# A decoder layer on one core: attention scores in four row groups of TensorE, the shared network by pairs of tiles, the expert loop three blocks deep

## The chip, the cores and the metric

The kernel runs on one core of a Trainium2 chip. The metric is the device time of one execution in microseconds (us), as the median of three runs. A core has five engines that run their own in-order programs and meet at semaphores: TensorE (PE) for matrix products, VectorE (DVE), ScalarE (ACT), GpSimd (POOL) and SyncE (SP), which issues transfers. Operands lie in SBUF; matrix products are written to eight banks of PSUM, each 128 partitions by 512 fp32 values.

## The reference

One layer on x of shape 8 x 128 x 256, with a context of the same shape. Cut to what matters:

```python
# 1. causal attention with low-rank queries and keys, 16 heads of 16 (2 of them rotary), per sequence of 128
h   = layernorm(x)
cq  = layernorm(h @ W_dq) * q_w + q_b            # 128 wide
ckv = layernorm(h @ W_dkv) * kv_w + kv_b         # 170 wide
q   = concat(cq @ W_uq, rope(cq @ W_qr))         # 14 + 2 heads
k   = concat((ckv @ W_ukv)[..., :224], rope(h @ W_kr))
v   = (ckv @ W_ukv)[..., 224:]
x   = x + softmax(mask(q @ k.T / 4)) @ v @ W_o.T
# 2. cross attention, 2 heads of 128; the scores are summed over the 8 sequences
Q, K, V = layernorm(x) @ Wh, ctx @ Wh, ctx @ Wh
A   = maximum(abs((Q @ K.T / sqrt(128) * decay).sum(axis=0)), 1)
x   = x + (relu(layernorm(x) @ Wg) * groupnorm(A @ V)) @ Wo
# 3. 16 experts of width 176, top 2 of each token's softmax, and a shared network of width 352
f   = layernorm(x);  p = softmax(f @ gate.T);  w, idx = top_k(p, 2)
x   = x + sum_k w_k * swiglu(f @ w_gu[idx_k]) @ w_dn[idx_k] + swiglu(f @ s_gu) @ s_dn
```

## The kernel before

A token tile is one sequence of 128 tokens (T = 128, B = 8 tiles, D = 256, which makes KD = 2 pieces of 128). Every engine has one program, written out by hand; the order of the work is the order of the calls in it, and waits on counted semaphores join the engines. A name such as `bank` stands for any PSUM bank.

**Attention.** The main loop of the PE program runs over the tiles i and does four chunks (NC = 4) of four heads (CH = 4). A chunk has three steps, a chunk or two apart: `scores` (L506), one product of K = 128 rows by 512 columns whose moving operand `kbd` is a block-diagonal spread of the keys of four heads, made by POOL's `expand` (L378); `prob_transpose` (L513), four transposes; `weigh_values` (L523), four products in which the transposed probabilities `prT` are the stationary operand and the 17 columns of `v_s` (16 values and a column of ones, which gives the softmax denominator) move. Between them DVE scales and masks the scores into `sc_s` (L1197) and takes the row maximum (L1200), and ACT does the exponentials (L939) and copies the transposed probabilities out of PSUM (L932). Interleaved are the steps of the tiles ahead and behind: `front_transpose` (L459) and `front_project` (L467) of tile i+2, `latent_transpose` (L472), `keys_values` (L483) and the query product (L485), `qk_transpose`, then `out_transpose` (L537) and `out_project` (L544) of tile i-1 or i-2, and for the cross attention `cross_transpose`, `cross_queries` (L559) and `cross_scores` (L567), which sums over all tiles in one bank. `ctx_part` makes the context's keys and values ahead of the loop. `gates` (L600) are the relu gates, in pairs of tiles q.

**Mixing.** After the last `cross_scores`, DVE applies the decay, `cross_mix(q)` multiplies by the context's values, group norm and gates follow on DVE, ACT and POOL, `cross_out` projects, and `cross_residual` adds x1 by a product with the identity. `router` makes the logits.

**Routing.** DVE finds the top two of 16 experts by a row of small operations from L1370 to `mb` (L1388); PE counts the pairs, DVE and POOL (L426) work out slots and rows. Each expert's rows are padded to blocks of 128; the program has 31 blocks, and the reference's inputs fill 25 of them. Meanwhile PE runs the shared network for the first six tiles (EARLY = 6): `shared_gate` (L747), `shared_up` (L753), `shared_transpose` (L762), `shared_down` (L771).

**Expert loop.** For each block POOL gathers 128 rows by an indirect transfer (L441), PE transposes them (L805), multiplies by the expert's weights (L821), transposes the hidden rows (L813) and multiplies down (L828); DVE copies the result (L1457), and POOL scatters it to `expert_out` in device memory (L446). After the loop PE does the last two tiles of the shared network, SP waits until all 31 blocks are scattered, and then loads each tile's two expert rows (L353):

```python
for r in range(RB):
    sp.wait_ge(dma_scattered[r], 16 * len(range(r, BLOCKS, RB)))
for t in range(B):
    sp.dma_start(yg[t], expert_out[0:SLOTS, :]...)   # L353, each tile's two rows
```

DVE weighs and adds them (L1495), and ACT's queue stores the output.

## Time and profile before

| | before |
|---|---|
| time, median of three runs | 334.25 us (333.32 to 335.49) |
| span of the profiled execution | 318.4 us |
| around the span (median less span) | 15.85 us |
| PE busy | 287.7 us, 90% of the span |
| DVE busy | 177.9 us, 56% |
| ACT busy | 136.5 us, 43% |
| POOL busy | 120.3 us, 38% |
| chain that ended last | PE 63%, DVE 15%, issue 9%, POOL 5%, DMA 4% |

The profile lists no time of its own for the profiled execution beside its span; the median of the runs stands for it. The span is what the engines' instructions cover, from the first to the last; the time of a run is longer by what lies around it. The chain is followed back from the last instruction to what released each step, so a share of it is time in which that engine set the end.

### The profile page before, as it was taken

Reading aid. Unit: us, or ns where it says so; the run is one execution under the profiler, and the core shown is the slowest. Engines: PE = TensorE matmul, PEld = TensorE weight load, DVE = VectorE, ACT = ScalarE, POOL = GpSimd, SP = SyncE. Lnnn points to the kernel's source line nnn. Section 1 sums busy time; section 2 is a strip of 40 time slices with the busy share of each in tenths; the row PEclk is TensorE's granted clock in tenths of the full one; section 3 lists DMA queues with packets and bytes.
Section 4 is the critical chain, followed back from the end, with each engine's and each line's share of the span. In section 5 each row is a group of like instructions: output and inputs, shape, how many; then the busy total and the mean of one; then the engine's idle time right before and its main releaser. Section 6 shows DMA issues by size and latency. Waiting matters only on the chain.

```text
span 318.4 us, 4990 instructions
## 1 busy us (share of the span) xinstructions
PE 287.7 (90%) x1492; PEld 209.9 (66%) x1493; DVE 177.9 (56%) x474; ACT 136.5 (43%) x363; POOL 120.3 (38%) x122
## 2 busy tenths in 40 slices
PE   2988798998999999999989899988999999999971
PEld 1645566676777677787877567656677777777750
DVE  1345666467587878556426873984433443334336
ACT  2555575536567575756631536321122222222220
POOL 1123333305133335051001730044677777776510
PEclk9999989587999999999999999999999999999995
DMA  7999872000000001000100012001323333333157
GB/s 225 261 332 369 248 185 88 2 0 0 2 0 3 1 0 30 2 1 3 45 1 2 0 66 68 0 0 37 98 92 108 99 109 102 102 99 99 49 176 252
DMA packets 20396, 26.72 MB, mean 84 GB/s; under 512 B 2640, under 2 KB 18138, under 8 KB 20378
## 3 DMA queue, kind: packets, MB, share of 16 engines
q1 hardware_dynamic: 16250, 17.31, 18.2%
q0 software_dynamic: 2976, 8.13, 8.6%
q10 hardware_dynamic: 1152, 1.05, 1.0%
q8 instruction: 10, 0.16, 0.2%
q14 instruction: 8, 0.07, 0.1%
HBM read 20.32 MB, written 6.16 MB: 83 GB/s over the span
## 4 chain that ended last, share of the span: by engine, by line
PE 63%; DVE 15%; issue 9%; POOL 5%; DMA 4%; ACT 2%; SPq 0%; DVEq 0%; POOLq 0%; ACTq 0%
PE bank L821 12%; PE bank L828 8%; PE bank L506 5%; PE bank L523 5%; PE bank L483 4%; PE bank L513 3%; PE bank L544 3%; PE bank L813 2%; PE bank L805 2%; DVE qk L1205 2%; PE bank L467 2%; DVE lat L1228 2%; PE bank L600 2%; POOL rs L371 2%; DMA cv_s<-expert_out 2%
## 5 line engine op out<-in xcount | busy, mean ns | idle before, releaser
L932 ACT ACTIVATE prT<-bank 128x512 f32<-128x512 f32 (+1 forms) x63 | 30.8, 489 | 74.8 <-PE bank L813 54.9
L939 ACT ACTIVATE pr_s<-sc_s,mx 128x128 f32<-128x128 f32 x128 | 40.8, 392 | 12.6 <-DVE mx L1200 12.6
L821 PE MATMUL bank<-gu_s,bxT 128*128 x124 | 41.9, 460 | 0.0
L1457 DVE COPY kbd<-bank 128x256 f32<-128x256 f32 x31 | 13.2, 425 | 42.8 <-PE bank L828 42.8
L366 POOL TENSOR_TENSOR rs<-ve,halfpow 128x1 f32<-128x1 f32 x16 | 8.8, 551 | 72.7 <-DVE ve L1177 72.7
L446 POOL DMA_INDIRECT expert_out<-kbd,prT x31 | 30.6, 986 | 15.0 <-DVE kbd L1457 7.7
L506 PE MATMUL bank<-kbd,qkT 128*128 128x512 f32 x64 | 36.0, 648 | 0.0
L441 POOL DMA_INDIRECT qx_s<-ffn_in,prT x31 | 30.1, 972 | 12.7 <-issue 7.3
L523 PEld LDWEIGHTS bank<-v_s,prT 128*128 128x128 f32 x256 | 32.2, 197 | 0.7 <-issue 0.7
L523 PE MATMUL bank<-v_s,prT 128*128 128x17 f32 x256 | 31.9, 258 | 0.3
L378 POOL TENSOR_TENSOR kbd<-qkT,tab 128x1024 f32<-128x1024 f32 x16 | 30.3, 1896 | 4.6 <-ACT qkT L932 4.6
L828 PE MATMUL bank<-dn_s,prT 88*128 x124 | 31.8, 379 | 0.0
L1197 DVE SCALAR_TENSOR_TENSOR sc_s<-bank,tabb 128x512 f32<-128x512 f32 x32 | 22.0, 687 | 14.4 <-PE bank L506 14.4
L513 PEld LDWEIGHTS bank<-tab,pr_s 128*128 128x128 f32 x128 | 17.3, 151 | 18.3 <-issue 17.9
L821 PEld LDWEIGHTS bank<-gu_s,bxT 128*128 128x128 f32 x124 | 21.2, 190 | 6.7
L1200 DVE TENSOR_REDUCE mx<-sc_s 128x4 f32<-128x512 f32 x32 | 21.9, 686 | 1.1
L828 PEld LDWEIGHTS bank<-dn_s,prT 88*128 88x128 f32 x124 | 21.1, 190 | 1.8
L371 POOL TENSOR_TENSOR rs<-ve,halfpow 128x2 f32<-128x2 f32 x8 | 5.6, 699 | 42.3 <-DVE ve L1220 42.3
L513 PE MATMUL bank<-tab,pr_s 128*128 128x128 f32 x128 | 20.7, 288 | 0.0
L483 PE MATMUL bank<-wkv_s,ckvT 85*128 85x480 f32 x32 | 16.4, 638 | 0.0
L771 PE MATMUL bank<-kbd 128*128 128x256 f32 (+1 forms) x48 | 12.1, 387 | 2.9 <-DVE x_s L1344 2.2
L467 PE MATMUL bank<-wm_s,xT 128*128 128x362 f32 x32 | 12.7, 522 | 1.2 <-ACT xT L932 1.0
(172 smaller groups left out, 492.7 us busy)
## 6 DMA issues: line engine op xcount, KB each, us to landing
gu_s<-in_w_gu SPq DMA_DIRECT2D x8, 704.0 KB, 10.4
dn_s<-in_w_dn SPq DMA_DIRECT2D x4, 704.0 KB
qx_s<-in_ctx_in SPq DMA_DIRECT2D x2, 512.0 KB, 7.5
ffn_in<-x_s SPq DMA_DIRECT2D x4, 256.0 KB, 2.1
cv_s<-expert_out SPq DMA_DIRECT2D x4, 256.0 KB, 3.9
gu_s<-expert_out SPq DMA_DIRECT2D x4, 256.0 KB, 5.4
out<-x_s ACTq DMA_DIRECT2D x8, 128.0 KB, 2.3
sgu_s<-in_s_gu_d SPq DMA_DIRECT2D x1, 704.0 KB, 6.7
```

Source lines behind the costliest of these rows:

```text
L378: nc.gpsimd.tensor_tensor(kbd[:, b % 2, g, :, :], qkT[:, b % 2, 2 + g, :].unsqueeze(1).to_broadcast([128, 8, T]), tab[:, C_HEAD:C_HEAD + 8 ...
L441: pool.indirect_dma_start(bx[:, i % RB, :], None, ffn_in[:], bass.IndirectOffsetOnAxis(ap=idx[:, 0, i:i + 1], axis=0)).then_inc(dma_gather ...
L446: pool.indirect_dma_start(expert_out[:], bass.IndirectOffsetOnAxis(ap=idx[:, 1, k:k + 1], axis=0), by[:, k % RB, :], None).then_inc(dma_sc ...
L483: last = mm(bank[3][:, 0:NOPE + D], ckvT[:, b % 2, k, :], wkv_s[:, k, :], start=k == 0, stop=k == 1)
L506: mm(o, qkT[:, b % 2, g, :], kbd[:, b % 2, g, h0:h0 + CH, :], start=True, stop=True).then_inc(pe_scores, 1)
L513: last = tr(bank[2][:, h * T:(h + 1) * T], pr_s[:, n % 2, h, :], idf)
L523: last = mm(bank[6][:, hh * (DH + 1):(hh + 1) * (DH + 1)], prT[:, n % 2, h, :], v_s[:, b % 3, hh, :], start=True, stop=True)
L821: last = mm(bank[2 + par][:, 0:2 * I], bxT[:, par, k, :], gu_s[:, k, bass.ds(e, 1), :], start=k == 0, stop=k == KD - 1)
L828: last = mm(bank[4 + par][:, 0:D], bhT[:, par, k, :], dn_s[:, k, bass.ds(e, 1), :], start=k == 0, stop=k == 1)
L932: copy = lambda o, i: nc.scalar.activation(o, i, ACT.Copy)
L939: last = nc.scalar.activation(pr_s[:, n % 2, h, :], sc_s[:, n % 2, h, :], ACT.Exp, bias=mx[:, n % 2, h:h + 1])
L1197: V.scalar_tensor_tensor(sc_s[:, n % 2, :, :], s, DH ** -0.5, maskb.unsqueeze(1).to_broadcast([128, CH, T]), ALU.mult, ALU.add).then_inc(d ...
```

## The change

- Scores: the 128 rows of queries and keys are taken as four groups of 32 rows. `kbd` spreads keys over two heads instead of eight and is made by DVE with the scale in it (`qk_out`), and a tile's scores are eight products of 32 rows by 256 columns, in four banks. The causal mask is put into the banks ahead of them by a bf16 product with the identity (`mask`). DVE only takes the row maximum from PSUM; ACT's exponentials read PSUM and give the denominators by `accum_out`.
- `weigh_values` has `v_s` as the stationary operand (32 columns, in one of four column groups) and the probabilities move, so its result comes out transposed. The reciprocals of the denominators are spread by POOL, transposed by PE (`rden_transpose`) and multiplied in. `out_transpose` is gone.
- x and the context also come transposed from the host; the front layer norm is folded into its weights (`weight_mean`). `cross_queries` is gone, since the context's keys are multiplied by Wh·Wh^T (`wh_square`). Half of the context's keys and values are made in tiles 0 and 1.
- `cross_scores` of all tiles stand behind the last tile; `gates` of pairs 0, 1 and 2 stand in the last two tiles, and those of pair 3 around the mixing. `cross_residual` is gone, DVE adds x1.
- Router: one column-tiled group of products (`routers`), a copy, two transposes; the top two are taken from the logits.
- Shared network: by pairs of tiles, hidden values made transposed, 256 columns per product, no transposes. Pairs 0 to 2 are done ahead of the loop, a third of pair 3 after block 14, the rest after the loop.
- Expert loop: written out, hidden rows two blocks and the down product three blocks behind `expert_up`; the copy of the result on ACT.
- SP waits only for the scatters of the blocks in use before it loads the token rows, and stores the outputs.

The core of the diff:

```diff
-                h0 = (c % 2) * CH
-                o = bank[n % 2][:].rearrange("p (h k) -> p h k", h=CH)
-                mm(o, qkT[:, b % 2, g, :], kbd[:, b % 2, g, h0:h0 + CH, :], start=True, stop=True).then_inc(pe_scores, 1)
+            def mask(b, r):
+                if b:
+                    pe.wait_ge(act_exp, NC * (b - 1) + r + 1)
+                mm(score_bank(r)[:].rearrange("p (h k) -> p h k", h=CH), idb, maskb.unsqueeze(1).to_broadcast([128, CH, T]),
+                   start=True, stop=False, skip_group_check=True)
+
+            def scores(b):
+
+                pe.wait_ge(dve_qk_T, b + 1)
+                for g in range(2):
+                    for r in range(NC):
+                        rows = slice(32 * r, 32 * r + 32)
+                        last = mm(score_bank(r)[:, g * 2 * T:(g + 1) * 2 * T].rearrange("p (h k) -> p h k", h=2),
+                                  qkT[rows, b % 2, g, :], kbd[rows, b % 2, g, :, :], start=False, stop=g == 1,
+                                  skip_group_check=True)
+                last.then_inc(pe_scores, 1)
...
-                    last = mm(bank[6][:, hh * (DH + 1):(hh + 1) * (DH + 1)], prT[:, n % 2, h, :],
-                              v_s[:, b % 3, hh, :], start=True, stop=True)
+                    v0 = (4 * half + h) * 2 * DH
+                    v0 = VB - DH + v0 if par else v0
+                    last = mm(bank[6][2 * DH * h:2 * DH * (h + 1), half * T:(half + 1) * T],
+                              v_s[:, b % 3].rearrange("p a n -> p (a n)")[:, v0:v0 + 2 * DH], prT[:, n % PR, h, :],
+                              start=c == 0, stop=c == NC - 1, skip_group_check=True)
...
+            def rden_transpose(b):
+                pe.wait_ge(pool_rden_spread, b + 1)
+                for k in range(KD):
+                    last = mm(bank[6][:, (KD + k) * T:(KD + k + 1) * T], rdx[:, k * T:(k + 1) * T], idf,
+                              start=False, stop=False, is_transpose=True, skip_group_check=True)
+                last.then_inc(pe_rden_T, 1)
...
+            def shared_up(q, c, halves=(0, 1)):
+
+                n, r = SC * q + c, shared_rows(c)
                 pe.wait_ge(act_ffn_in_T, q + 1)
...
+                for j in halves:
                     for k in range(KD):
+                        last = mm(shared_bank(q, c)[0:r, 2 * j * T:2 * (j + 1) * T],
+                                  sgu_s[:, k, j * SI + c * 128:j * SI + c * 128 + r],
+                                  xfT[:, k, 2 * q:2 * q + 2, :].rearrange("p b t -> p (b t)"), start=k == 0, stop=k == KD - 1)
...
+            for i in range(2, BLOCKS):
+                hidden_transpose(i - 2)
+                expert_up(i)
+                if i + 2 < BLOCKS:
+                    block_transpose(i + 2)
+                if i >= 3:
+                    expert_down(i - 3)
+                if i + 1 < BLOCKS:
+                    read_expert(i + 1)
+                if i == MID:
+                    shared_up(PAIRS - 1, 0)
...
                 for h in range(CH):
-                    last = nc.scalar.activation(pr_s[:, n % 2, h, :], sc_s[:, n % 2, h, :], ACT.Exp,
-                                                bias=mx[:, n % 2, h:h + 1])
+                    d0 = n % NC // 2 * 8 + 2 * h + n % 2
+                    last = nc.scalar.activation(pr_s[:, n % 2, h, :], score_bank(n)[:, h * T:(h + 1) * T], ACT.Exp,
+                                                bias=mx[:, n % 4, h:h + 1], accum_out=den[:, n // NC % 2, d0:d0 + 1])
...
+            sp.wait_ge(dve_ring, 1)
+            written = [sp.value_load(ring_i[0:1, r:r + 1], min_val=16, max_val=16 * len(range(r, BLOCKS, RB))) for r in range(RB)]
             for r in range(RB):
-                sp.wait_ge(dma_scattered[r], 16 * len(range(r, BLOCKS, RB)))
+                sp.wait_ge(dma_scattered[r], written[r])
```

TensorE's program in a steady attention tile. Before, between the scores of a chunk and the next but one; `bank<-kbd,qkT` are scores, `tab,pr_s` the transposes of the probabilities, `v_s,prT` the weighing:

```order
L506 MATMUL bank<-kbd,qkT 128x512
L513 MATMUL bank<-tab,pr_s 128x128 x4
L523 MATMUL bank<-v_s,prT 128x17 x4
L483 MATMUL bank<-wkv_s,ckvT 128x480 x2
L485 MATMUL bank<-wq_s,cqT 128x288
L459 MATMUL bank<-tab,xh 128x128 x2
L506 MATMUL bank<-kbd,qkT 128x512
L513 MATMUL bank<-tab,pr_s 128x128 x4
L523 MATMUL bank<-v_s,prT 128x17 x4
L544 MATMUL bank<-wout_s,oT 128x256 x2
```

After, from the second chunk's transposes of a tile to the scores of the next; `tabb` is the mask product, `prT,v_s` the weighing, `tab,lat` and `tab,xb` transposes:

```order
L547 MATMUL bank<-tab,pr_s 128x128 x4
L582 MATMUL bank<-wout_s,oT 128x256 x2
L491 MATMUL bank<-tab,lat 128x128
L493 MATMUL bank<-tab,lat 85x128 x2
L547 MATMUL bank<-tab,pr_s 128x128 x4
L559 MATMUL bank<-prT,v_s 32x128 x8
L528 MATMUL bank<-tabb 128x512
L594 MATMUL bank<-tab,xb 128x128 x2
L506 MATMUL bank<-wkv_s,ckvT 128x480 x2
L512 MATMUL bank<-wq_s,cqT 128x288
L528 MATMUL bank<-tabb 128x512
L537 MATMUL bank<-kbd,qkT 128x256 x8
```

The scores of a tile stand together at its start and the weighing goes two chunks at a time; every chunk's transposes are a place of their own.

VectorE's program in the routing, from the first maximum of the logits. Before:

```order
L1370 TENSOR_REDUCE s<-bank 128x8
L1371 TENSOR_TENSOR qkT<-bank,s 128x128
L1373 TENSOR_REDUCE s<-qkT 128x8
L1374 RECIPROCAL s<-s 128x8
L1375 TENSOR_TENSOR qkT<-qkT,s 128x128
L1378 TENSOR_REDUCE s<-qkT 128x8
L1379 TENSOR_TENSOR qkT<-qkT,s 128x128
L1380 SCALAR_TENSOR_TENSOR qkT<-qkT,tab 128x128
L1381 TENSOR_REDUCE s<-qkT 128x8
L1382 TENSOR_TENSOR qkT<-tab,s 128x128
L1339 TENSOR_TENSOR kbd<-bank,kbd 128x352
```

After, as far as `mb`:

```order
L1446 TENSOR_REDUCE s<-bank 128x8
L1447 TENSOR_TENSOR qkT<-bank,s 128x128
L1438 SCALAR_TENSOR_TENSOR qkT<-qkT,tab 128x128
L1439 TENSOR_REDUCE s<-qkT 128x8
L1440 TENSOR_TENSOR qkT<-tab,s 128x128
L1449 SCALAR_TENSOR_TENSOR qkT<-qkT,bank 128x128
L1450 TENSOR_REDUCE s<-qkT 128x8
L1451 TENSOR_TENSOR qkT<-qkT,s 128x128
L1438 SCALAR_TENSOR_TENSOR qkT<-qkT,tab 128x128
L1439 TENSOR_REDUCE s<-qkT 128x8
L1440 TENSOR_TENSOR qkT<-tab,s 128x128
L1453 TENSOR_TENSOR mb<-qkT 128x128
```

The softmax of the logits (ACT's exponentials behind L1371, the sum and the division) no longer stands ahead of the choice, and no product of the shared network stands inside the row.

## Rows read from the trace of the kernel before

**Rows 1.** Windows, the whole program by stage: start:end, length, busy (instructions), clock, DMA, GB/s

```profile
core 0: us, PE busy (x) PEld busy (x) DVE busy (x) ACT busy (x) POOL busy (x), PEclk, DMA share, GB/s
0.00:26.51 26.51, 18.89 (x84) 12.41 (x86) 8.75 (x33) 11.66 (x23) 6.19 (x13) 1.00 0.95 282
26.51:169.83 143.32, 134.27 (x733) 98.28 (x731) 92.30 (x219) 84.26 (x234) 38.63 (x34) 0.94 0.16 48
110.58:126.73 16.15, 15.38 (x93) 11.46 (x92) 13.01 (x32) 10.73 (x31) 6.48 (x6) 1.00 0.06 15
169.83:197.48 27.65, 25.75 (x136) 20.06 (x137) 18.15 (x57) 12.27 (x20) 10.81 (x12) 1.00 0.12 39
197.48:223.79 26.31, 23.31 (x143) 16.54 (x141) 19.11 (x53) 6.70 (x19) 8.12 (x7) 1.00 0.06 16
223.79:301.00 77.21, 77.02 (x370) 56.87 (x369) 30.65 (x91) 19.70 (x62) 54.63 (x56) 1.00 0.32 95
301.00:318.40 17.40, 8.44 (x36) 5.73 (x34) 8.92 (x21) 1.91 (x6) 1.94 (x2) 0.81 0.63 203
...
55.20:66.00 10.80, 10.80 (x29) 6.45 (x29) 5.23 (x12) 5.17 (x15) 2.42 (x2) 0.53 0.01 2
```

**Rows 2.** Chain that ended last, a steady tile: start, us, engine, output, line, count

```profile
110.75 0.86 PE bank L506 x2
111.61 0.44 PE bank L513 x4
112.05 0.80 PE bank L523 x8
112.85 1.71 PE bank L483 x4
...
117.36 0.97 PE bank L544 x4
...
137.59 0.86 PE bank L600 x4
```

**Rows 3.** Timeline of PE: start, us, instruction, [wait before it and what ended it]

```profile
55.02 0.33 PE L472 MATMUL bank<-tab,lat 128*128 128x128 f32 x1 [0.87 <-DVE qk L1205]
...
125.91 0.33 PE L472 MATMUL bank<-tab,lat 128*128 128x128 f32 x1 [0.77 <-DVE qk L1205]
```

**Rows 4.** Groups of VectorE and ScalarE in 110.58:126.73: busy us, mean ns, idle before

```profile
L1200 DVE TENSOR_REDUCE mx<-sc_s 128x4 f32<-128x512 f32 x5 | 3.4, 686 | 0.2
L1197 DVE SCALAR_TENSOR_TENSOR sc_s<-bank,tabb 128x512 f32<-128x512 f32 x4 | 2.7, 686 | 0.2 <-PE bank L506 0.2
L1180 DVE TENSOR_SCALAR xh<-x_s,ag,rs 128x256 f32<-128x256 f32 x1 | 1.4, 1383 | 0.0
...
L939 ACT ACTIVATE pr_s<-sc_s,mx 128x128 f32<-128x128 f32 x16 | 5.1, 393 | 1.0 <-DVE mx L1200 1.0
L932 ACT ACTIVATE prT<-bank 128x512 f32<-128x512 f32 x4 | 2.4, 594 | 2.9 <-PE bank L513 2.9
```

**Rows 5.** Groups of PE over the whole span, the bf16 products of the routing

```profile
L785 PE MATMUL bank<-mb,onesb 128*128 128x16 bf16 x8 | 0.3, 169 | 0.0
L783 PE MATMUL bank<-mb,tabb 128*128 128x128 bf16 x1 | 0.2, 216 | 0.0
```

**Rows 6.** Chain that ended last, the routing, from the logits to the first expert product

```profile
197.48 0.30 DVE s L1370
...
203.36 0.30 DVE mb L1388
...
218.44 1.20 POOL qx_s L441
...
219.93 3.52 DMA qx_s<-ffn_in,prT
```

**Rows 7.** Chain that ended last, the end of the program

```profile
302.37 2.42 DMA expert_out<-kbd,prT
...
306.37 4.90 DMA cv_s<-expert_out
```

More of the change, by code:

```diff
@@ L685, in _ @@
+                if tiles(i - 2) and i < B - 1:
+                    cross_transpose(i - 2)
+                if tiles(i + 2):
+                    keys_values(i + 2)
+                    queries(i + 2)
+            prob_transpose(NC * B - 1)
+            weigh_values(NC * B - 2)
+            weigh_values(NC * B - 1)
+            rden_transpose(B - 1)
             cross_transpose(B - 2)
-            gates(1, 1)
-            out_transpose(B - 1)
-            cross_queries(B - 2)
+            cross_scores(0)
@@ new lines, in shared_down @@
+            def shared_down(q):
+                pe.wait_ge(dve_shared_hidden, SC * (q + 1))
+                if q >= 2:
+                    pe.wait_ge(dve_shared_added, q - 1)
+                for b in range(2):
+                    for c in range(SC):
+                        r = shared_rows(c)
+                        last = mm(bank[shared_out(q)][:, b * D:(b + 1) * D], shT[0:r, q % 2, c, b * T:(b + 1) * T],
+                                  sdn_s[0:r, c, :], start=c == 0, stop=c == SC - 1)
@@ new lines, in _ @@
+            expert_down(BLOCKS - 2)
+            expert_down(BLOCKS - 1)
+            shared_up(PAIRS - 1, 1)
+            shared_up(PAIRS - 1, 2)
+            for c in range(SC):
+                pe.wait_ge(dve_shared_hidden, SC * (PAIRS - 1) + c + 1)
+                r = shared_rows(c)
+                for b in range(2):
+                    last = mm(last_pair_out(b), shT[0:r, (PAIRS - 1) % 2, c, b * T:(b + 1) * T], sdn_s[0:r, c, :],
+                              start=c == 0, stop=c == SC - 1)
+                    if c == SC - 1:
+                        last.then_inc(pe_shared_down, 1)
@@ L1123, in _ @@
-            shared_silu(1)
-            for b in range(EARLY):
-                if b >= 1:
-                    shT_out(b)
-                if b + 2 < EARLY:
-                    shared_silu(b + 2)
-            def silu(i, par, first=False):
+            shared_silu(0, 1)
+            shared_silu(0, 2)
+            act.wait_ge(pe_logits_T, 1)
+            copy(lgT, bank[5][:, 0:2 * T]).then_inc(act_logits_T, 1)
+            for c in range(SC):
+                shared_silu(1, c)
+            shared_silu(2, 0)
@@ L1137, in hT_out @@
-            def hT_out(i, par, first=False):
+                nc.scalar.activation(bs[:, i % 2, :], bank[2 + i % 2][:, 0:I], ACT.Silu).then_inc(act_expert_silu, 1)
+            def hT_out(i):
                 act.wait_ge(pe_hidden_T, i + 1)
-                if not first:
+                if i >= 2:
                     act.wait_ge(pe_expert_down, i - 1)
-                copy(bhT[:, par, :, :].rearrange("p k t -> p (k t)"), bank[1][0:IH, 0:2 * T]).then_inc(act_hidden_T, 1)
-            silu(0, 0, True)
@@ new lines, in _ @@
+            silu(0)
+            silu(1)
+            for i in range(2, BLOCKS):
+                hT_out(i - 2)
+                silu(i)
+                if i >= 3:
+                    y_out(i - 3)
+                if i == MID:
+                    shared_silu(PAIRS - 1, 0)
+            hT_out(BLOCKS - 2)
+            y_out(BLOCKS - 3)
+            hT_out(BLOCKS - 1)
+            y_out(BLOCKS - 2)
+            y_out(BLOCKS - 1)
+            shared_silu(PAIRS - 1, 1)
+            shared_silu(PAIRS - 1, 2)
```

1260 lines of the change are left out of this document (626 added, 634 removed).

## The prediction, as put on record before the changed kernel ran

> **What bounds the kernel now.** I read the windows by stage first, then the chain, then the groups. PE is busy 134.27 of 143.32 us in the attention, 77.02 of 77.21 in the expert loop and 23.31 of 26.31 in the routing [rows 1]: a product that is taken away there is time, so long as its operands are there. In a steady tile, 16.15 us between two latent transposes, PE is busy 15.38 and waits 0.77, for DVE's last query step [rows 1, 3]; DVE is busy 13.01, ACT 10.73, POOL 6.48. Three things are not PE's. The start has 7.6 us in which PE idles under a DMA share of 0.95. The routing's chain goes over DVE, the gather (1.20 + 3.52) and back [rows 6]. The end, 17.40 us, has PE busy for 8.44; the last scatter (2.42) and the load of the token rows (4.90) stand in it [rows 7]. And the granted clock: mean 0.94 in the attention, 0.53 in 55.20 to 66.00, after a wait of 0.87 us, so at its lower level of 1.2 GHz; the wait of 0.77 at 125.91 was not followed by a fall [rows 1, 3]. The clock costs 143.3 x 0.06 = 8.6 us there.
>
> The median is 334.25 for a span of 318.4. I work in spans and add 15.85.
>
> **Prices.** 512 fp32 columns are 0.86 (two instructions), so 256 are 0.43, which four instructions for two products of 256 confirm (0.86); a transpose is 0.11, 480 columns twice 1.71, two output products 0.97 [rows 2]. By the same 0.84 us per 500 columns the query product of 288 is 0.49 and the two of 362 are 1.22. A chunk's weighing is 0.80 for eight instructions. The mask is bf16: from 16 to 128 columns a product grew from 169 to 216 ns [rows 5], 0.42 ns per column, so 0.215 for 512; it can't be under 0.2, nor over the fp32 0.86.
>
> **A, the start (26.51).** PE loses the transposes of the context (16 x 0.11 = 1.8) and of x (0.4), half the context's keys and values (two of 512 columns, 1.7, and 8 of 128 with two instructions each, 1.7): 5.6. It gains the mean of the weights (1.2), Wh squared (0.4), three masks (0.65) and the keys, values and queries of tile 1 (2.2): 4.5. Net -1.1, and the weights that the first product needs now stand first in their queue, on two queues where one was. Of the idle 7.6 I take 2.1 back: -3.2. Bounds 0 (the loads end it as now) and -6 (little idle left).
>
> **B, the attention (143.32).** PE's work in a steady tile: 27 transposes (16 of probabilities, 3, 4, 2 and 2) 2.9; four masks 0.86; scores; weighing; latents 1.22; keys and values 1.71; queries 0.49; output 0.97. Front transposes, output transposes and Wh's product are gone. Scores are 16 instructions of 256 columns: 0.215 x 16 = 3.4 in a row, as now; a quarter, 0.86, if four row groups run at once. Two instructions of one product must follow each other in the same group, so with the neighbouring group beside them I take 1.9. The weighing, 8 instructions of 128 columns a chunk, is 0.86 in a row, 0.22 four at once; I take 0.54, 2.1 a tile. No row shows two products side by side, so both ends stay in the range. Sum 12.2, against 15.38.
>
> Then the waits. All scores of a tile stand together, ahead of the maximum (0.69 of DVE per chunk) and four exponentials (about 0.32 apart, 1.3 in all [rows 4]). Between scores and the first chunk's transposes PE has about 3 us of other work for a path of max, exponentials and copies; I put 1.1 us of wait there, 0.5 ahead of `out_project` (reciprocal, POOL, transpose, copy, normalise) and 0.2 at the latents: 14.0, and 0.2 for PE's changes between whole array and groups. So **14.2** a tile. DVE: four masks-and-scales (2.7) go, so do the copies for x (its 1.38 was beside POOL's spread) and come two spreads and the latents' copies: about 11 us. ACT: 5.1 for exponentials plus what the accumulator costs, no copies of x, queries or output; 8.5 to 11.3. Both stay under 14.2, ACT as second. POOL's 16 spreads are off its path.
>
> The Trainium skill, "TensorEngine Tiling (Array Packing)", Key Properties, says that changing the tiling mode drains TensorE. There are six to eight changes in a tile. The row nearest to it is a transpose after a wait, 0.33 against 0.11 in a row [rows 2, 3], so at most 0.22 each, 1.7 a tile; hidden where PE waits at that place anyway, which is why I keep 0.2. By the page's rule at full price the tile would be 15.7, and the kernel 12 us slower than I say.
>
> Tiles: 1.9 (first scores) + 15.6 (tile 0, with context) + 15.0 (tile 1) + 4 x 14.2 + 12.0 (tile 6: no latents or keys ahead, 3.8 less, two gates more, 1.7) = 101.3. From the last scores to `cross_mix` PE has gates of two pairs 3.4, transposes 1.8, weighing 2.1, eight `cross_scores` 3.5, the last gate 0.9, the rest 3.0: 14.7; the chain of the last tile through reciprocals, output, norm and copy leaves 3.4 of wait: 18.1. B = 119.4, plus the clock. I take 6 lost of the 8.6 of before, since a tile now has waits as long as those ahead of a fall; bounds 0 and all attention at the lower level (below). B = 125.4: **-17.9**.
>
> **C, mixing (27.65).** Four residual products (4 x 0.86 = 3.4) and `gates` copies leave; `routers` all at once (8 products of 256 columns, 3.4 in a row, 0.9 with four column groups at once), its copy and the two transposes come behind the last norm, where before only the last pair's small products were. DVE now adds x1 on the chain of the last pair. PE isn't the bound at its end. I take -0.5, bounds -3.4 and +2.
>
> **D, routing (26.31).** To `mb` 6.2 us before, 19 steps; now 12 at 0.325 each (0.30 and its start) = 3.9 [rows 6]. One of POOL's two products for the slot table goes to ACT, which halves the longest step beside it, and shared work is in pairs: hot rows at 12.3, table 13.5, rows 15.6, gather and transposes as before from issue to product 5.35 (223.79 - 218.44): 21.1, **-5.2**. The cover ran out first before: PE was busy 23.31. Now three pairs have 12 products of 256 columns up and 6 down each, 54 x 0.43 = 23.2, of which three `shared_up` (5.2) stand in C: 18.0 and the counts and slots fit under 21.1, with little to spare. Bounds -7 and 0.
>
> **E, loop and end (77.21 + 17.40 = 94.6).** The loop holds the same 31 x 2.49; three blocks deep instead of two removes no work, since PE idled 0.2 in all. `shared_up` in block 14 adds 1.72: 78.9. POOL's two indirect transfers a block are 54.63 busy of 77.21, so PE still leads. After it: before, two shared tiles and scatter, load 4.90, sums. Now the load waits only for blocks in use, 25 of 31, so it lies under the last blocks; PE does two thirds of `shared_up` (3.4), its silu and product (about 1.3), six downs of two (2.6), then sum, store and its landing (about 3.8): 11.1. E = 90.0, **-4.6**. Bounds: -8 (the thirds overlap) and +1 (stores in line behind SP's waits). What is queued behind SP's new wait are only loads and stores of the outputs.
>
> **Sum:** -3.2 - 17.9 - 0.5 - 5.2 - 4.6 = -31.4; span 287.0, time 302.9. I say **302**.
>
> **Rivals.**
> (1) Groups don't overlap: the change doesn't do what it says. Scores 3.4 and weighing 3.4 for 1.9 and 2.1, +2.8 a tile, of which the waits swallow 0.7: +17 in eight tiles, 319. For: no row shows overlap. Against: outputs lie in different banks and groups. 0.16.
> (2) They overlap more and the waits are shorter: scores 1.1, weighing 1.4, a wait less and a steady clock, -12: 291. For it speaks that PE's work goes down to 10.7 a tile; against, that then DVE's 11 and ACT's 8.5 to 11.3 bound it. 0.24. The Trainium skill, "TensorE: Matmul & The Clock Gate", Part 3, Measured speedup, has 3.07 times for four row tiles and 2.38 for three column tiles, which gives such numbers; no run here shows it yet.
> (3) The clock: each tile has a wait of about 1 us, and [rows 3] show a fall after 0.87. At half speed 10.8 us cost 0.47 x 10.8 = 5.1. If 30 us of the attention lie there, 14 against my 6: 310. 0.12.
> (4) Slower: the same mechanism with no recovery, since every tile brings the next wait. A microsecond at the lower level loses 0.47; to eat the 31.4 beyond the 12.8 us counted already it needs 67 more, so from about 80 of 119 us at the lower clock it decides. With all tiles there: +45, 347. Before, PE always came back within 10.8 us. 0.02.
> The forecast itself, all parts within some 7 us: 0.46.
>
> **How the numbers follow.** The likeliest case gives 302. To hold 8 in 10, the range takes in (2) and (3) and half of (1): 286 to 319. What a measurement of this kernel can tell from no change is about 1%, 331 to 337.6. Faster needs only a tenth of the sum: cases 0.46, 0.24, 0.16, 0.12 all lie there, less 0.04 for a stall that I don't see (a wait on a landing, a bank that comes free late) of 30 us: faster 0.95, same 0.03, slower 0.02.
>
> **What would show each step.** The tile's length between two latent transposes (14.2), PE busy in it (12.2), the eight score products in the chain (1.9, or 3.4, or 1.1) and the weighing per chunk (0.54, 0.86, 0.35); ACT's mean per exponential (393 now; over 500 would make ACT the bound); the granted clock by tile; first scores at 23.3; from the logits to `mb` 3.9, to the first L872 21.1; PE's loop at 78.9 with POOL under it; first load of token rows ahead of PE's last block. I would be wrong by much if exponentials read slowly from PSUM, if the chain ran over ACT in the attention, or if the clock stayed low.

## The result, and the profile after

The changed kernel took 281.75 us (281.48 to 284.15, four runs) against 334.62 for the kernel before: a ratio of 0.845, interval 0.840 to 0.851. The forecast was 302, range 286 to 319: faster, as forecast, but by 53 us where 32 were forecast, and outside the range. Run again later (experiment `after_again`) it took 271.74 us against 318.92, ratio 0.869 (0.857 to 0.882). A ratio with an interval compares only the faster executions of each kernel, so it needn't be the quotient of the medians beside it.

The stages of the changed kernel, from the windows view of its first profile. They answer to [rows 1]; the third row is a steady tile.

```profile
core 0: us, PE busy (x) PEld busy (x) DVE busy (x) ACT busy (x) POOL busy (x), PEclk, DMA share, GB/s
0.00:24.37 24.37, 17.46 (x66) 10.43 (x66) 10.15 (x40) 7.14 (x16) 3.42 (x8) 1.00 0.98 282
24.37:132.21 107.84, 97.08 (x791) 62.97 (x791) 73.77 (x221) 72.53 (x320) 12.70 (x22) 1.00 0.28 80
77.74:90.12 12.38, 11.53 (x97) 7.06 (x97) 10.12 (x33) 8.93 (x40) 1.84 (x4) 1.00 0.01 1
132.21:159.61 27.40, 23.88 (x131) 18.71 (x132) 20.34 (x64) 9.55 (x18) 10.84 (x12) 1.00 0.11 39
159.61:180.61 21.00, 19.36 (x130) 15.71 (x129) 17.62 (x51) 6.04 (x11) 7.07 (x6) 1.00 0.08 20
180.61:271.36 90.75, 82.90 (x379) 58.40 (x380) 25.59 (x75) 29.82 (x93) 55.00 (x57) 1.00 0.34 99
271.36:280.10 8.74, 6.04 (x28) 4.74 (x27) 4.80 (x12) 1.15 (x3) 2.14 (x2) 1.00 0.64 230
```

| stage | before | forecast | first profile | run again |
|---|---|---|---|---|
| A, to the first scores | 26.51 | 23.3 | 24.37 | 23.76 |
| B, attention | 143.32 | 125.4 | 107.84 | 107.86 |
| C, mixing | 27.65 | 27.1 | 27.40 | 27.38 |
| D, routing | 26.31 | 21.1 | 21.00 | 21.05 |
| E, loop and end | 94.6 | 90.0 | 99.49 | 89.15 |
| span | 318.4 | 287.0 | 280.1 | 269.2 |
| time less span | 15.85 (assumed) | 15.85 | 1.9 | 1.8 |

C and D came as forecast, A within 1.1 us. Two things are far off in the span, and they pull against each other: the attention is 17.6 us shorter than forecast, and in the first profile loop and end are 9.5 us longer. The third is outside the span: I added 15.85 us, and the changed kernel has 1.9.

A steady tile in the chain that ended last (start, us, engine and line). It answers to [rows 2]: scores are `L537`, transposes of probabilities `L547`, weighing `L559`, output `L582`, masks `L528`, keys and values `L506`.

```profile
77.74 1.08 PE bank L537 x16
78.81 0.60 PE bank L547 x4
...
79.93 1.10 ACT pr_s L980 x6
...
81.48 0.66 PE bank L547 x4
82.14 0.57 PE bank L559 x16
82.71 0.60 PE bank L522 x4
...
83.68 0.76 DVE kbd L1216 x2
...
84.57 1.10 PE bank L582 x4
...
87.77 1.66 PE bank L506 x4
```

All scores of a tile take 1.08 us where they took 3.44; the weighing of two chunks 0.57 where one took 0.80. The chain now goes over ACT's exponentials once (three of them with their accumulator reads, 1.10) and over DVE's `qk_out` once (0.76), which is new beside [rows 3].

In the first profile the expert loop took 90.75 us. Less the 1.73 of `shared_up` in it that is 2.87 a block, where PE's work is 2.49. The timeline of PE and then of ACT in one stretch of it:

```profile
204.92 1.35 PE L872 MATMUL bank<-gu_s,bxT 128*128 x4
206.10 0.38 PE L855 MATMUL bank<-tab,qx_s 128*128 128x128 f32 x2
206.32 1.03 PE L882 MATMUL bank<-dn_s,prT 88*128 x4
207.81 0.39 PE L863 MATMUL bank<-tab,pr_s 128*88 128x128 f32 x2 [0.46 <-ACT prT L970]
```

```profile
205.86 0.38 ACT L970 ACTIVATE by<-bank 128x256 f32<-128x256 f32 x1 [1.73 <-PE bank L882]
207.29 0.38 ACT L970 ACTIVATE prT<-bank 88x256 f32<-88x256 f32 x1 [1.05 <-remote]
210.91 0.32 ACT L1144 ACTIVATE pr_s<-bank 128x176 f32<-128x176 f32 x1 [3.24 <-PE bank L872]
211.12 0.38 ACT L970 ACTIVATE by<-bank 128x256 f32<-128x256 f32 x1
211.39 0.38 ACT L970 ACTIVATE prT<-bank 88x256 f32<-88x256 f32 x1
```

By the trace the product that ends at 206.27 is what the silu at 210.91 waited for: 4.6 us lie between them, and then ACT works off a backlog. The same pattern returns at 223.3, 235.7 and 248.1. No engine's work explains this wait, and the first experiments were to settle it.

### The profile page after: what moved, and what is told of

The parts are those of the page before. It is cut to its first block, busy times and chain, and to the rows that moved or that the text cites. A ratio compares the mean times of both kernels' runs of the same rounds, so it can differ in the third digit from the quotient of the medians.

```text
span 280.1 us, 4960 instructions
## 1 busy us (share of the span) xinstructions
PE 246.7 (88%) x1518; PEld 171.0 (61%) x1518; DVE 152.3 (54%) x460; ACT 126.2 (45%) x461; POOL 91.2 (33%) x106
## 4 chain that ended last, share of the span: by engine, by line
PE 71%; DVE 9%; ACT 7%; issue 6%; another core or an unknown queue 2%; DMA 1%; POOL 1%; ACTq 0%; POOLq 0%; DVEq 0%
PE bank L872 13%; PE bank L882 8%; PE bank L805 7%; PE bank L547 5%; PE bank L506 5%; ACT pr_s L980 4%; PE bank L537 3%; PE bank L559 3%; PE bank L818 3%; PE bank L582 3%; PE bank L863 3%; PE bank L855 2%; ACT prT L970 2%; DVE kbd L1216 2%
## 5 line engine op out<-in xcount | busy, mean ns | idle before, releaser
L980 ACT ACTIVATE pr_s<-bank,mx 128x128 f32<-128x128 f32 x128 | 46.6, 420 | 0.0
L1525 DVE TENSOR_TENSOR pr_s<-bank,pr_s 128x176 f32<-128x176 f32 x31 | 10.6, 341 | 61.6 <-ACT pr_s L1144 49.5
L464 POOL DMA_INDIRECT expert_out<-by,prT x31 | 31.0, 1000 | 26.9 <-ACT by L970 19.5
L980 ACT ACTIVATION_READ_ACCUMULATOR pr_s<-bank,mx 128x1 f32 x128 | 33.5, 261 | 0.0
L872 PEld LDWEIGHTS bank<-gu_s,bxT 128*128 128x128 f32 x124 | 21.1, 190 | 10.8 <-issue 4.3
L547 PE MATMUL bank<-tab,pr_s 128*128 128x128 f32 x128 | 20.3, 281 | 7.1 <-ACT pr_s L980 4.7
L547 PEld LDWEIGHTS bank<-tab,pr_s 128*128 128x128 f32 x128 | 13.8, 141 | 17.0 <-ACT pr_s L980 9.7
L970 ACT ACTIVATE by<-bank 128x256 f32<-128x256 f32 x31 | 11.9, 385 | 25.1 <-PE bank L882 16.4
L1206 DVE TENSOR_REDUCE mx<-bank 128x4 f32<-128x512 f32 x32 | 19.9, 684 | 4.1 <-PE bank L537 4.1
L805 PE MATMUL bank<-ck_s,sgu_s 128*128 128x256 f32 (+1 forms) x96 | 22.0, 380 | 0.0
L393 POOL TENSOR_TENSOR rs<-ve,halfpow 128x1 f32<-128x1 f32 x8 | 4.4, 548 | 49.2 <-DVE ve L1191 49.2
L805 PEld LDWEIGHTS bank<-ck_s,sgu_s 128*128 128x128 f32 (+1 forms) x96 | 17.1, 181 | 3.4 <-issue 0.4
L863 PE MATMUL bank<-tab,pr_s 128*88 128x128 f32 x62 | 12.0, 274 | 7.1 <-ACT prT L970 4.9
L1519 DVE COPY bxT<-bank 128x256 f32<-128x256 f32 x31 | 12.9, 417 | 4.9 <-PE bank L855 4.9
L506 PE MATMUL bank<-wkv_s,ckvT 85*128 85x480 f32 x32 | 14.4, 572 | 0.5 <-ACT ckvT L1020 0.5
## 6 DMA issues: line engine op xcount, KB each, us to landing
gu_s<-in_x_t SPq DMA_DIRECT2D x1, 768.0 KB, 12.5
```

Of the source, the lines that this page charges most:

```text
L464: pool.indirect_dma_start(expert_out[:], bass.IndirectOffsetOnAxis(ap=idx[:, 1, k:k + 1], axis=0), by[:, k % RB, :], None).then_inc(dma_sc ...
L506: last = mm(bank[3][:, 0:NOPE + D], ckvT[:, b % 2, k, :], wkv_s[:, k, :], start=k == 0, stop=k == 1)
L547: last = tr(bank[2][:, h * T:(h + 1) * T], pr_s[:, n % 2, h, :], idf)
L805: last = mm(shared_bank(q, c)[0:r, 2 * j * T:2 * (j + 1) * T], sgu_s[:, k, j * SI + c * 128:j * SI + c * 128 + r], xfT[:, k, 2 * q:2 * q + ...
L863: last = tr(bank[1][0:IH, k * T:(k + 1) * T], bh[:, i % 2, k * IH:(k + 1) * IH], idf)
L872: last = mm(bank[2 + i % 2][:, 0:2 * I], bxT[:, i % 2, k, :], gu_s[:, k, bass.ds(e, 1), :], start=k == 0, stop=k == KD - 1)
```

## The experiments

**The kernel before, again.** No edit.

> The kernel before, unchanged, to see what lies between its span and its time. The changed kernel's four runs each have a time 1.7 to 1.9 us over their span, so if that holds for any kernel, this one has a span of 332 to 333 us in a run of 334, with a granted clock under that of the profile shown (span 318.4), whose execution would then have taken about 320. The rival: some 15 us lie around the span of this kernel in every run, and the change took them away; then the span is near 318 again with a time near 334.

Span 318.2 in a run of 320.0; eight runs of it and thirteen of the kernel beside it lie between 312.5 and 321.2 us, each 1.8 us over its span. So what lies around the span is 1.8 us, for this kernel as for the changed one. Neither branch of the expectation was right in full: the span is near 318, and so is the time. If the three runs of 333 to 335 also had 1.8 us around them, their spans were near 332, and they were longer executions than the profiled one of 318.4, by some 14 us. Their spans aren't known. The granted clock in the 21 runs was 0.962 to 0.989, and the shortest had the highest.

**Scores row group by row group.**

```diff
-                for g in range(2):
-                    for r in range(NC):
+                for r in range(NC):
+                    for g in range(2):
```

> The eight score products of a tile are issued row group by row group (both products of a group in a row) instead of round the four groups. If it is the side-by-side running of four groups that makes the 16 instructions take 1.08 us, they take over 2 us now, near 2 to 3.4, and the kernel is slower by 0.5 to 1.5 us a tile, 4 to 12 us in all. If the 1.08 comes from 32 rows being cheaper than 128, whatever the order, nothing moves.

272.64 us (270.77 to 274.30), a ratio of 0.852 (0.845 to 0.858) to the kernel before. The 16 instructions take 1.10 us, a tile 12.36. The order of the products over the groups doesn't matter here. The expectation took that as a sign that 32 rows are cheap in themselves, but four groups that run at once in either order would look the same; `e_one_group` below tells the two apart. The run showed something else. Its loop has no late signals; 183.20 to the end, 272.3, is 89.1 us, against 99.5 in the first profile, and its loop code is the same.

**SP waits for all scatters, by constants.**

```diff
-                sp.wait_ge(dma_scattered[r], written[r])
+                sp.wait_ge(dma_scattered[r], 16 * len(range(r, BLOCKS, RB)))
```

> SP waits for the scatters of all 31 blocks by constants, as before the change, and reads no counts. In the loop of the changed kernel PE's signals come up to 4.6 us late in bursts, about once in four blocks (12.4 us). Theory 1, SP's wait on a register's value disturbs them: the bursts go, the loop falls from 90.8 to about 79 us, while the load of the token rows moves behind the last scatter and costs some 5 to 8 us at the end; in all -4 to -6 us. Theory 2, the copy of the expert's result on ACT stands in the way of the silu and hidden copies behind it: the loop stays at 90.8 and the time grows by 5 to 8 us.

285.17 us (283.03 to 287.69), ratio 0.889 (0.882 to 0.895). No late signals here either, but none in the other two runs on this chip, which keep SP's wait on a register: that wait alone doesn't bring them. What the run prices is the end. Loop and end are 100.55 us (182.95 to 283.5) against 89.10 in `e_scores_row` on the same chip, 11.4 more, where 5 to 8 were expected for the load. The medians differ by 12.5, but in that are 1.2 each by which attention and mixing were longer in this profile, at granted clocks of 0.98 and 0.94, and first scores that came 2.6 earlier. The chain at the end, which answers to [rows 7]:

```profile
264.69 2.42 DMA expert_out<-by,prT
...
267.25 0.36 SPq L372
...
270.22 5.68 DMA x_s<-expert_out
...
276.86 4.00 PE bank L963 x8
...
280.88 0.42 DVE x_s L1559
```

Scatter, SP's issues, load, sums and then the last shared products at the lower clock (0.50 granted from 276.86 to 280.86; eight instructions in 4.00 us, where twelve take 2.61 below), after PE had mostly stood still: all of that is gone from the chain where SP waits for the used blocks only.

**The copy of the expert's result back on DVE.** The call, cut out of both engines' programs:

```diff
-                if i >= 3:
-                    y_out(i - 3)          # ScalarE's loop
+                if i >= 3:
+                    y_out(i - 3)          # VectorE's loop, behind h_mul and bT_out
```

> The copy of each block's result goes back from ACT to DVE, with the same waits, behind that step's two other copies. Theory 2 (the copy, which waits for an old scatter, holds up ACT's silu and hidden copy): the loop falls from 90.8 to about 79 us, the kernel is faster by 10 to 12 us. Theory 1 (SP's register wait) and any cause on PE or the queues: the bursts of late signals stay, the loop stays within 1 or 2 us of 90.8.

274.95 us (274.51 to 278.33), ratio 0.864 (0.857 to 0.871), 2.3 over `e_scores_row` on the same chip. The loop runs at 2.49 a block, as with the copy on ACT. Theory 2 falls: ACT's copy costs the loop nothing. Loop and end are 93.23 us against 89.10 there, 4.1 longer (the medians differ by less, since first scores came at 23.61 and not at 26.81). They are lost at the end, where DVE copies the last three blocks ahead of the token sums, and PE waits for DVE's products of the last pair (2.9 us in all).

**The changed kernel, again.** No edit.

> The changed kernel, unchanged, beside its variants and the kernel before. The variant with the scores' order changed had a loop and end of 89.1 us without late signals, where the changed kernel's first profile had 99.6 with them. Theory: the late signals belong to where or when that execution ran, not to the kernel, so the loop and end are near 89 now and the span near 270. Rival: they belong to this kernel's code and the variants' small edits removed them by chance; then 99 again and a span near 280.

271.74 us (270.95 to 274.17), span 269.2. Stages, windows view:

```profile
0.00:23.76 23.76, 17.42 (x66) 10.26 (x66) 10.15 (x40) 7.15 (x16) 3.43 (x8) 1.00 0.97 283
23.76:131.62 107.86, 97.09 (x792) 62.94 (x791) 73.72 (x221) 72.67 (x320) 12.73 (x22) 1.00 0.29 82
...
180.05:269.20 89.15, 85.63 (x406) 63.76 (x406) 30.31 (x86) 31.41 (x96) 57.43 (x59) 1.00 0.40 123
```

and the end of the chain, which is PE alone:

```profile
258.57 1.84 PE bank L882 x8
260.40 3.46 PE bank L805 x16
263.86 2.61 PE bank L964 x12
...
266.49 0.42 DVE x_s L1560
```

A to D are those of the first profile within 0.7 us; only the loop differs, by 10.3. So the same kernel runs with late signals on one occasion and without them on another. None of the other profiles made later has them. Whether they need something of this kernel as well as the occasion isn't shown.

**All scores in one row group.**

```diff
-                        rows = slice(32 * r, 32 * r + 32)
+                        rows = slice(0, 32)
```

> All eight score products of a tile read rows 0 to 31, so all lie in one row group; the scores are then those of the first two heads of each half, and the output is not the layer's. If four groups running at the same time make the 16 instructions take 1.08 us, they take 16 x 0.215 = 3.4 now: 2.4 us more a tile, less what PE waited anyway (0.85), 12 to 19 us in all. If a product of 32 rows is simply cheaper, it stays at 1.08.

299.00 us (296.73 to 302.54), ratio 0.953 (0.936 to 0.969). The chain has

```profile
60.82 3.65 PE bank L537 x16
75.73 3.65 PE bank L537 x16
```

3.65 us for what takes 1.08 over four groups, 3.4 times as long, and a tile of 14.91 for 12.36. The two rows are from stretches at full clock. The attention grew by 26.0 us (133.89), 5.6 more than eight times 2.55: its mean clock was 0.94. So products of 32 rows aren't cheap in themselves; they are cheap because four groups run at once.

**The weighing of three chunks in one column group.**

```diff
-                    last = mm(bank[6][2 * DH * h:2 * DH * (h + 1), half * T:(half + 1) * T],
+                    o = 0 if c else h
+                    last = mm(bank[6][2 * DH * o:2 * DH * (o + 1), half * T:(half + 1) * T],
```

> Of the weighing, the products of chunks 1 to 3 of each tile all write column group 0, so four of one chunk can't run at once; the output is not the layer's. If column groups run at the same time, a chunk's weighing goes from 0.285 to 0.86 us: 3 x 0.57 = 1.7 us more a tile, 7 to 14 us in all. If not, no change.

291.02 us (290.07 to 292.09), ratio 0.930 (0.920 to 0.939). The chain of a tile has 1.86 for two such chunks and 1.21 for one beside an unchanged one, 0.93 a chunk against 0.285:

```profile
77.51 1.86 PE bank L560 x16
83.23 1.21 PE bank L560 x16
```

A tile is 14.18, 1.82 longer; the attention 122.97, 15.1 longer, a little over the 7 to 14 expected. Column groups run at the same time too. In one group the four products also write the same 32 rows of the bank, and no run separates that from the group itself. The rest of the 19 us isn't the weighing's: first scores came 2.5 us later, and loop and end took 92.15, 3.0 more. With an output that isn't the layer's the tokens go to other experts, and the load of the token rows began 75.8 us after the first expert product where it was 73.3.

**Exponentials without their denominators.**

```diff
-                                                bias=mx[:, n % 4, h:h + 1], accum_out=den[:, n // NC % 2, d0:d0 + 1])
+                                                bias=mx[:, n % 4, h:h + 1])
```

> The exponentials give no denominators; a constant stands in for them, so the output is not the layer's. The trace has 128 accumulator reads of 0.26 us each, 33.5 us of ACT. If they stretch the path from the row maximum to the transposes (three exponentials in 1.10 us, four in 1.50 where four took 1.3 before the change), the attention is shorter by 0.2 us per chunk on the chain, one or two chunks a tile: 1.5 to 4 us in all. If ACT is the bound of a tile, it is more, up to 8 us. If PE alone is, nothing.

271.86 us (271.30 to 272.11), ratio 0.868 (0.861 to 0.875). The time is that of the changed kernel, but the stages aren't: the attention is 104.8 (26.15 to 130.92) instead of 107.86, while the first scores came at 26.15, behind a load of 11.34 us (`e_wkv_first` below), and the mixing took 28.58 for 27.38, at a granted clock of 0.94. A steady tile:

```profile
66.39:78.37 11.98, 11.30 (x98) 7.12 (x97) 10.08 (x33) 7.65 (x24) 1.81 (x4) 1.00 0.00 1
```

0.38 less than 12.36, 3 us in all, in the middle of the 1.5 to 4 expected: the reads are on the chain once or twice a tile, and ACT isn't its bound.

**The changed kernel, a third time.** No edit.

> The changed kernel, unchanged, beside the next three on the same chip. If the late signals in the expert loop belong to the place of an execution, a chip that runs the kernel before at 319 runs this one near 271 without them; where the kernel before takes 334, they show again and it takes 281.

273.99 us (271.15 to 275.50) with the kernel before at 320.52. Attention 107.88, loop and end 89.22, no late signals; the first scores at 27.05, and the mixing 28.57 at a granted clock of 0.94. The second branch, an occasion with 334 for the kernel before, didn't come up again.

**The gates behind the last tile.**

```diff
-                if i == B - 2:
-                    pe.wait_ge(ld_wg_wo, 48)
-                    gates(0, 0)
-                    gates(0, 1)
...
             cross_scores(B - 1)
+            pe.wait_ge(ld_wg_wo, 48)
+            for q in range(3):
+                gates(q, 0)
+                gates(q, 1)
             gates(3, 0)
```

> The gates of pairs 0 to 2 (three times 1.7 to 1.9 us of PE) go from the last two attention tiles to behind the last cross scores, and their relu on VectorE with them. If they filled time in which PE would have waited for exponentials and copies, tiles 6 and 7 and their tail get shorter by less than the 5.5 us that they took, and the kernel is slower by 5 to 8 us (three gates, and up to three relus of 0.9 that PE must wait for). If PE bounds those tiles whatever stands there, the tiles give all 5.5 back and only the relus' 2.7 show.

280.22 us (279.44 to 283.16), 6.2 over `after_third` on the same chip. Tile 6 is 9.84 us with its gates and 9.84 without them. Tile 7's timeline without them:

```profile
118.73 0.66 PE L547 MATMUL bank<-tab,pr_s 128*128 128x128 f32 x4 [1.87 <-ACT pr_s L974]
...
120.98 0.69 PE L547 MATMUL bank<-tab,pr_s 128*128 128x128 f32 x4 [1.02 <-ACT prT L964]
121.47 1.92 PE L582 MATMUL bank<-wout_s,oT 128*128 128x256 f32 x4
...
135.97 1.97 PE L638 MATMUL bank<-qx_s,wg_s 128*128 128x256 f32 x8 [0.87 <-DVE qx_s L1273]
```

Waits of 1.87 and 1.02 stand where gates stood, the output product behind them takes 1.92 instead of 1.10 (the lower clock, 0.50 granted from 121.47 to 124.50), and the gates are paid in full at the end, with three waits of 0.87 or 0.88 for VectorE's relu. From the scores of tile 7 to `cross_mix` it is 27.9 us instead of 19.9. So the place of the gates is worth 8 us in this execution, the slowest of the four, in which the clock fell in tile 7, and 6.2 by the medians.

**No mask.**

```diff
-                mm(score_bank(r)[:].rearrange("p (h k) -> p h k", h=CH), idb, maskb.unsqueeze(1).to_broadcast([128, CH, T]),
-                   start=True, stop=False, skip_group_check=True)
```

> The causal mask is left out, so each token sees its whole sequence and the output is not the layer's. Theory 1, PE's work bounds a steady tile (11.5 of 12.36 us busy): it falls by the four masks, 0.86, to about 11.5, and the kernel by 7 us. Theory 2, the chain scores, maximum, exponentials, transposes, weighing, normalising bounds it: less than half of that, 0 to 3 us.

277.60 us (276.61 to 278.01), slower than `after_third` by 3.6. A steady tile and the start of the expert loop:

```profile
67.44:79.57 12.13, 10.63 (x93) 6.68 (x93) 10.08 (x33) 8.93 (x41) 1.81 (x3) 1.00 0.01 3
181.88:192.00 10.12, 9.51 (x29) 6.00 (x30) 3.56 (x11) 1.71 (x5) 4.72 (x5) 0.66 0.25 66
```

PE's work fell by 0.90 in the tile, the tile by 0.23. What is missing came back as two new waits of PE, 0.43 for ACT's copy of the transposed probabilities and 0.22 for DVE's `ckvT`: the masks had stood in front of them. So it isn't PE's work alone that bounds a steady tile, and theory 2 holds.

The loss is elsewhere. Attention as a whole was 0.8 us shorter than in `after_third` (its clock fell to 0.66 in 45 to 50 us), loop and end were 5.1 longer, 94.32. Of these, 10.12 x 0.34 = 3.4 us lie in the second row: the clock was 0.66 in the loop's first 10 us, in a stage that the edit doesn't touch. The rest is at the end, whose chain goes over a scatter (2.42) and the load of the token rows (6.08) instead of PE alone; the tokens' experts are others than the layer's here too. All four runs had a mean clock of 0.966 to 0.972, so the time isn't one bad run's. The fall in the loop goes with the landing of the first gather. PE's wait for it, in the first profile and in this one:

```profile
179.02 0.44 PE L855 MATMUL bank<-tab,qx_s 128*128 128x128 f32 x2 [0.28 <-DMA qx_s<-ffn_in,prT]
```

```profile
180.30 0.44 PE L853 MATMUL bank<-tab,qx_s 128*128 128x128 f32 x2 [0.59 <-DMA qx_s<-ffn_in,prT]
```

Behind it come waits of 1.15 and 0.60 in both; every profile of the changed kernel and its variants has 1.14 to 1.24 and 0.60 there. In the three whose clock fell at the loop's start the first wait was 0.42 (`e_wkv_first`), 0.59 (this one) and 0.67 (`e_one_group`); in the nine others it was 0 to 0.32. No run changes that wait on purpose, so this is a pattern and not a shown cause.

**Weights of keys and values loaded earlier.**

```diff
             sp.dma_start(wht_s, wh_t.rearrange("h p n -> p h n")).then_inc(ld_wh_t, 16)
+            sp.dma_start(wkv_s[:], w_kv.rearrange("(k p) n -> p k n", p=KPH)).then_inc(ld_w_kv, 16)
             sp.dma_start(cT[:, :, 0:4, :], ctx_in[:, :, 0:4, :]).then_inc(ld_ctx0, 16)
```

> The weights of keys and values are loaded ahead of the context and of x's second part. In some executions PE waits at the start for these weights (until 14.9 us) and the first scores come at 26.1 instead of 23.7 us, with the clock at its lower level behind the wait. If their place in the queue is the cause, all executions have first scores at 23.7 or earlier, 0 to 2.4 us gained; if the loads as a whole are, the wait moves to the context's load and nothing is gained.

276.77 us (275.39 to 278.90), 2.8 over `after_third`; first scores at 27.86, 0.8 later. Loop and end are 91.77 against 89.22, with the clock's fall at the loop's start described above. The chain of the start, `after_third` and then this one:

```profile
3.64 12.13 DMA wkv_s<-in_w_kv
...
15.86 3.47 PE bank L506 x4
```

```profile
3.36 11.38 DMA x_s<-in_x
```

The wait moves to the next load, x's second part. The loads as a whole end this stage in such executions (DMA share 0.97 and 0.98), and this order among them gains nothing.

No variant was faster than the changed kernel by more than the spread of the runs.

## Why the prediction was wrong, step by step

**The constant.** "The median is 334.25 for a span of 318.4. I work in spans and add 15.85": this step failed. Every run since lies 1.8 to 1.9 us over its span, and a time of 334 goes with a longer execution than the one profiled. The sum of the spans, 287.0, would have given 288.8. The page had no time of the profiled execution, and I let the median stand for it.

The constant isn't what was wrong about the change, though. Where both kernels ran on one occasion it cancels: the medians fell by 47.2 us (`after_again`) and 46.5 (`after_third`), the span from 318.4 to 269.2, that is by 49.2, where 31.4 were forecast. Of the 17.8 us missing between these spans 17.5 are the attention's. That is the step that failed.

**B, the attention.** Forecast 125.4, measured 107.84 and 107.86. By terms:

- Scores: 1.9 taken between 0.86 and 3.4, measured 1.08. Weighing: 2.1 a tile taken, measured 1.14. Together 1.8 less a tile, and the tile is 12.35 where 14.2 was forecast. I reasoned that the two instructions of an fp32 product must follow each other and so leave only the neighbouring group beside them. The 1.08 refutes that, and `e_scores_row` goes further: with all four instructions of a group in a row it takes the same time.
- The four steady tiles gave 7.4 us, tiles 0 and 1 1.9, tile 6 2.2. The tail, 18.1 and the 1.9 of the scores, was right (19.9).
- The clock: 6 us taken as lost, none measured in the attention of the first two profiles. That isn't for want of waits. In a steady tile they are short (PE idles 0.85 in all, the longest wait is 0.64), but tile 1 has one of 2.08 us in every profile with accumulator reads, longer than the 0.87 of [rows 3]. In the first profile, and then in `e_sp_const`, whose attention is the same code:

```profile
44.69 0.66 PE L547 MATMUL bank<-tab,pr_s 128*128 128x128 f32 x4 [2.08 <-ACT pr_s L980]
```

```profile
44.49 1.12 PE L546 MATMUL bank<-tab,pr_s 128*128 128x128 f32 x4 [2.08 <-ACT pr_s L979]
```

  The granted clock from 45 to 50 us was 1.00 in the first and 0.71 in the second. Of eleven profiles with this wait the clock fell behind it in four (`e_sp_const`, `e_one_group`, `e_one_column`, `e_no_mask`). So my premise, a wait and then a fall, holds in some executions and not in others, and that the first two lost nothing is in part luck: `e_sp_const` lost about 1.2 us.
- What bounds a tile: I summed PE's work to 12.2 and added 1.8 of waits and 0.2 for changes. Measured are 11.53 and 0.85. Scores and weighing took 1.8 less than in my sum, but the rest of PE's work took 9.3 where I had 8.2, since four transposes behind scores or weighing take 0.60 to 0.66 and not 0.44; and the waits were 0.95 shorter. The last two nearly cancel, which is luck. `e_no_mask` shows besides that 0.90 us of PE's work can be worth 0.23: adding PE's work up is right only for pieces that no other wait stands behind.

Rival (2) is what happened: wider overlap, fewer waits, a steady clock; -12 by my price, -17.5 as measured. The price left out a part of its own terms: 0.8 and 0.7 a tile for scores and weighing are the 12 already, and the steady clock that it names is 6 more. Rival (1), no overlap, is what `e_one_group` and `e_one_column` made: +26 us in the attention, 5.6 of it beyond the growth of the tiles, and +15 with three of four chunks. These count from the full overlap and my 17 from the middle values, but the change rests on the overlap more than I said. The Trainium skill, "TensorE: Matmul & The Clock Gate", Part 3, Measured speedup, gives 3.07 for four row tiles; here it is 3.65 / 1.08 = 3.4. I had the page's figure and weighed it as a rival, and took a middle value for want of a row; the end that the page stood at was the right one.

On changes of the tiling mode the rows are these: four transposes take 0.44 us behind whole-array work and 0.60 behind scores or weighing, also where all scores lie in one row group (`e_one_group`). That is 0.16 a change, at two or three places of a tile where PE didn't wait anyway, so near 0.4 where I took 0.2; the 1.7 of the full price would have been far too much. The Trainium skill, "TensorEngine Tiling (Array Packing)", Key Properties, has changing the mode drain the engine, and these rows agree with it, though no run separates the drain from other causes.

**A, C, D.** -3.2, -0.5 and -5.2 were forecast; -2.1, -0.3 and -5.3 came in the first profile. A depends on the execution: the first scores came between 23.6 and 27.9 us in the profiles, behind the loads. In D the row of small operations to `mb` took 3.86 (159.00 to 162.86 in the second profile) for 3.9.

**E, loop and end.** Forecast 90.0. It was 89.15 and 89.22 in the later profiles of the kernel, and the mechanism was right: a loop of PE's work with 1.73 for `shared_up`, loads hidden under the last blocks, a tail of PE alone. Two terms were off and offset each other: in the second profile the loop took 80.35 for 78.9 and what comes after it 8.80 for 11.1. The first profile had 99.49, by late signals that I had no row for. The gain of the ring counts alone is 11.4 us (`e_sp_const`), more than the whole -4.6 of the stage: without them loop and end would be 100.55, longer than the 94.6 of before. Beside scatter and load, the last shared products at the lower clock behind a standing PE are in it.

**Together.** 302.9 forecast less 281.75: the constant 14.0, attention 17.6, against 9.5 more in loop and end and 1.3 more in A, C and D: 20.8 of the 21.1. The late signals hide part of the attention's error in this time: without them it would have been 272.3, 30.6 under the forecast.

## What stays open

What made PE's signals late in the loop of the first profile, and whether the same made the kernel before take 334 us on that occasion. The later profiles, eleven of the changed kernel and its variants and one of the kernel before, on three chips, have neither. And why the same wait is followed by a fall of the clock in one execution and not in the next, in tile 1 and at the loop's start.

## What to carry to other kernels

Check the difference between time and span with two executions before adding it to a sum: it was 1.8 to 1.9 us in every run, and a median of longer executions than the profiled one hid 14 us in it. Small-K or small-M products over four groups of the array are worth pricing at the end where they all run at once, if they write different banks or partitions; the order in which row groups were issued didn't matter here. A single profile without a fall of the clock doesn't show that a kernel is free of it. To see whether PE's work or a chain bounds a stage that is 93% busy, take away a piece of its work that nobody waits for: here 0.90 us gave 0.23, while gates put into PE's waits of the last tile saved 6 to 8. A variant whose output is wrong can change later stages too, where they depend on the data, so compare it stage by stage.

## What the runs showed of the hardware

- An exponential with `accum_out` is two instructions on ScalarE; the second, from the page of the changed kernel, takes 0.26 us:

```profile
L980 ACT ACTIVATE pr_s<-bank,mx 128x128 f32<-128x128 f32 x128 | 46.6, 420 | 0.0
...
L980 ACT ACTIVATION_READ_ACCUMULATOR pr_s<-bank,mx 128x1 f32 x128 | 33.5, 261 | 0.0
```

  Three pairs take 1.10 us in a row, four 1.50; four without took 1.3 before [rows 4].
- Four row groups ran 16 fp32 instructions of 256 columns in 1.08 to 1.10 us in either order; one group took 3.65. Four column groups took 0.285 a chunk, one 0.93.
- Behind a PE that stood still for 1.9 and 1.0 us (`e_gates_late`), four instructions took 1.92 instead of 1.10 at a granted clock of 0.50; behind the load at the end of `e_sp_const`, eight took 4.00 where twelve take 2.61.
- A fall doesn't follow each wait: behind the 2.08 us in tile 1 the clock fell in four profiles and stayed at its full level in seven.
